# A graph network's fused build-and-update stage: the known half of the update is copied into the PSUM bank ahead of the products that add to it, and the relu reads the bank

## What is computed

```
h = relu(layernorm(x))
# block 0, message passing
m   = relu([h[src], h[dst], edge_attr] @ mW1 + mb1) @ mW2 + mb2
agg = segment_sum(m, src)
u   = relu([h, agg] @ uW1 + ub1)              # the stage of this change
x   = x + h + (u @ uW2 + ub2)
# block 1, three graph convolutions with the same edges and self loops
h = relu(layernorm(x))
x = x + gcn(gelu(gcn(gelu(gcn(h, W1, b1)), W2, b2)), W3, b3)
```

## Time and profile before

| | us |
|---|---|
| median of 3 runs | 2052.21 |
| lowest and highest run | 2049.65, 2060.61 |
| profiled execution | 2049.62 |
| its span, first to last instruction | 2047.8 |
| `build_and_update` in it | about 1218 to 1529 |
| `graph_layers` in it | about 1529 to the end |

### The profile page before, as it was taken

One profiled execution on the slowest core, in us unless ns is written; L12 is line 12 of the kernel. 1 busy time (PEld: TensorE's weight loads), 2 busy tenths in 40 slices (PEclk: granted clock), 3 DMA queues, 4 the chain that ended last, 5 costly groups with the idle time before them and its releaser, 6 DMA issues. The chain is left out here.

```text
span 2047.8 us, 34486 instructions
## 1 busy us (share of the span) xinstructions
PE 1817.7 (89%) x8786; PEld 1237.3 (60%) x8786; DVE 1542.7 (75%) x4650; ACT 797.9 (39%) x1975; POOL 1262.3 (62%) x1463
## 2 busy tenths in 40 slices
PE   4577887777399999999999998989979999999999
PEld 2344544444255555555555556666657888788887
DVE  7887787777489999999999988988988345445333
ACT  0122222222155665665665656656664112113000
POOL 2777777777788888888888859999979000000000
PEclk7677777888699999999999999999999999999999
DMA  5111111111276766666766785222236344343333
GB/s 163 39 58 51 52 58 58 58 58 56 69 197 195 198 195 195 198 195 195 196 196 194 194 173 163 69 66 68 72 92 185 93 124 124 93 126 121 109 108 110
DMA packets 181705, 254.12 MB, mean 124 GB/s; under 512 B 29244, under 2 KB 144761, under 8 KB 181514
## 3 DMA queue, kind: packets, MB, share of 16 engines
q0 software_dynamic: 47888, 126.25, 22.6%
q1 hardware_dynamic: 104696, 102.31, 16.4%
q10 hardware_dynamic: 28930, 23.35, 3.5%
HBM read 202.35 MB, written 49.37 MB: 123 GB/s over the span
## 5 line engine op out<-in xcount | busy, mean ns | idle before, releaser
L1009 POOL DMA_INDIRECT brow<-B_rows,rows x440 | 467.8, 1063 | 114.9 <-issue 58.4
L380 POOL DMA_INDIRECT src_list<-ring,ring_row x392 | 385.8, 984 | 156.7 <-issue 117.6
L1959 PE MATMUL pO<-F,y 128*128 128x512 f32 x1728 | 431.5, 404 | 4.7 <-DVE y L1770 3.2
L1959 PEld LDWEIGHTS pO<-F,y 128*128 128x128 f32 x1728 | 326.7, 190 | 79.8 <-DVE y L1770 4.0
L1332 POOL TENSOR_SCALAR src_oh<-iota,src_s 128x128 bf16<-128x128 bf16 x426 | 285.1, 685 | 39.9 <-PE pC L1475 21.8
L1059 PE MATMUL pNode<-hid_whole,oh 128*128 128x512 f32 x440 | 228.7, 601 | 4.9 <-DVE sums L1195 4.5
L1125 ACT ACTIVATE turned<-pC 128x256 fp32r<-128x256 bf16 x220 | 84.7, 385 | 279.9 <-PE pC L1038 279.9
L1348 DVE TENSOR_SCALAR dst_oh<-iota_cw,dst_s 128x458 bf16<-128x458 f16 x568 | 181.7, 366 | 0.0
L1061 PE MATMUL pNode<-hid_upper,oh 128*128 128x512 f32 x220 | 175.3, 797 | 0.0
L1475 PE MATMUL pC<-dst_oh,src_oh 128*128 128x458 bf16 x568 | 157.4, 361 | 16.6 <-SPq L1430 8.3
L824 PE MATMUL pP<-U,upto 128*128 128x182 bf16 x385 | 49.6, 280 | 136.4 <-DVE posf L587 136.4
(11 more groups left out here) (306 smaller groups left out, 3413.1 us busy)
## 6 DMA issues: line engine op xcount, KB each, us to landing
raw<-C_rows SPq DMA_DIRECT2D x54, 768.0 KB, 4.4
C_rows<-c_rows ACTq DMA_DIRECT2D x175, 114.5 KB, 1.7
raw_first<-C_rows SPq DMA_DIRECT2D x18, 768.0 KB, 4.4
rows<-src_list SPq DMA_DIRECT2D x110, 100.0 KB, 2.8
brow<-B_rows,rows POOLq DMA_INDIRECT x440, 3.8
U_parts<-part_u SPq DMA_DIRECT2D x25, 256.0 KB, 2.0
B_rows<-bst SPq DMA_DIRECT2D x25, 256.0 KB, 2.1
src_list<-ring,ring_row POOLq DMA_INDIRECT x392, 2.2
```

The costliest lines, as they stand in the source:

```text
L380: nc.gpsimd.indirect_dma_start(dr.src_list[:, :, :].rearrange("p t w -> (p t) w"), bass.IndirectOffsetOnAxis(ap=ring_row[:, k % RING, t:t ...
L1009: nc.gpsimd.indirect_dma_start(brow[:, t % BR, :], None, dr.B, bass.IndirectOffsetOnAxis(ap=rows_i[:, m % LCS, j, 1:2], axis=0)).then_inc( ...
L1959: last = mm(pO[m % 2][half][:, :], y[:, win, part, half * P:(half + 1) * P], F[:, n % FS, :], start=(win == 0 and part == 0), stop=False)
```

## The change

Before the 25 tiles begin, PE opens the bank `pU` with one product of 128x512 (in turn 1 at u = 1), which writes every column of it. Then, for each tile, DVE copies the known half from SBUF into `pU` at u == 3, after the relu of the tile before has read the bank; the products of `hidden` add to what stands in the bank (start=False) and no longer overwrite it; and the relu reads the bank directly. PE's first product of `hidden` waits for the copy (`known_ready`) in place of the relu (`u_ready`). The add at u == 8 is gone.

```diff
+        u_opened = g.sem("u_opened")
+        known_ready = g.sem("known_ready")
@@ vector engine
+                    if u == 3 and 0 <= i - 1 < NW:
+                        w = i - 1
+                        if w == 0:
+                            dve.wait_ge(u_opened, 1)
+                        else:
+                            dve.wait_ge(u_ready, w)
+                        dve.wait_ge(h_in[0 if w < HG else 1], 16 * (HG if w < HG else NW - HG))
+                        v.tensor_copy(pU[:, :].rearrange("p (b n) -> p b n", b=2), known_u(w)).then_inc(known_ready, 1)
@@ vector engine, u == 8
                         dve.wait_ge(u_done, w + 1)
                         if w >= 1:
                             dve.wait_ge(x_done, w)
-                        dve.wait_ge(h_in[0 if w < HG else 1], 16 * (HG if w < HG else NW - HG))
-                        link(v.tensor_tensor(uT.rearrange("p (b n) -> p b n", b=2),
-                                             pU[:, :].rearrange("p (b n) -> p b n", b=2), known_u(w), ALU.add))
-                        v.tensor_scalar(uT, uT, 0.0, None, ALU.max).then_inc(u_ready, 1)
+                        v.tensor_scalar(uT, pU[:, :], 0.0, None, ALU.max).then_inc(u_ready, 1)
@@ tensor engine, hidden
                     pe.wait_ge(at_ready, w + 1)
-                    if w >= 1:
-                        pe.wait_ge(u_ready, w)
-                    else:
-                        pe.wait_ge(steps_ready, 4)
+                    pe.wait_ge(known_ready, w + 1)
                 for k in range(2):
                     last = mm(pU[:, m * P:(m + 1) * P], uw1[:, 2 * (m // 2) + k, (m % 2) * P:(m % 2 + 1) * P],
-                              aggT[:, k * P:(k + 1) * P], start=(k == 0), stop=(k == 1))
+                              aggT[:, k * P:(k + 1) * P], start=False, stop=False, skip_group_check=True)
@@ tensor engine, the turns
+                    if i == 1 and u == 1:
+                        pe.wait_ge(steps_ready, 4)
+                        mm(pU[:, :], fresh[:, 0:P], fresh[:, 0:HID], start=True, stop=True).then_inc(u_opened, 1)
```

## The result

| | before | changed |
|---|---|---|
| median of 19 runs, us | 2053.81 | 2047.67 |
| lowest and highest run | 2048.87, 2060.61 | 2043.72, 2056.90 |
| profiled execution | 2049.62 | 2054.11 |
| first to last step of the stage | 308.6 | 304.5 |

The ratio is 0.997, its 95% interval 0.9957 to 0.9983: 6 us less, 3.5 to 9. That is inside what was forecast, in sign and in size, and less than 0.5%.

The account below looks back on a forecast made before the run. PE, DVE and POOL each near 90% busy, none alone the bound; PE and DVE tied in a loop. Terms -8.9 + 3.8 = -5.1 us gave 2044.5 to 2047.1, forecast 2046 us, range 2038 to 2054.

Parts of the forecast that it names:

- The loop: PE and DVE, one-hots to `update`: path 0.74 us instead of 1.22, capped by PE's idle time, 8.9 us less.
- The copy's price: DVE's 128x512 f32 copy from SBUF into PSUM: 650 ns taken, 450 to 680 kept as bounds.
- The copy's place: Copy at u == 3 delays the one-hots of u = 5 to 7 and `hidden`: 3.8 us given back.
- ACT's floor: ACT's bucket reads, 1.63 us each: a faster PE gains nothing in the tail, only in the 21 updates before.
- The sum: Whole kernel: -8.9 + 3.8 = -5.1 us, forecast 2046 us.
- (A): Rival: DVE's idle time hides the copy wholly and the tail gains too, 2037 to 2042 us; chance 0.22.
- (B): Rival: late one-hots after the copy cost PE about 10 us, the gain is gone, 2050 to 2053; chance 0.16.
- (C): Rival: DVE becomes the bound, all 24 turns pay 0.65 us, slower at 2057 to 2062; chance 0.07.
- (D): Rival: the seed in the bank is overwritten, time equals the forecast's; chance inside the forecast's 0.55.

Follow-up runs that it names:

- the relu alone: Changed kernel without the copy into the bank and the product that opens it, known half left out of the result: stage 301.1 us, ratio 0.9972.
- the copy alone: Kernel before, add kept, plus a DVE copy into the bank at u == 3 that the products overwrite: stage 314.4 us, ratio 1.0029.
- seven steps of lead: DVE's one-hots 7 steps ahead of PE in place of 5: stage 302.3 us in the changed kernel, 308.3 in the one before.
- half the copy: Kernel before, add kept, plus a copy at u == 3 of the first 256 columns only, overwritten by the products: stage 311.2 us.
- the copy at u == 1: Changed kernel with copy at u == 1, relu ahead of the one-hots of u == 8, one-hots 7 steps ahead: stage 295.6 us, ratio 0.9936.

## Why the prediction was right, and where it was not

- *The loop.* 0.48 us a turn was worked out, from 1.22 to 0.74; the turn shown has 0.72, and unit 0 is shorter by 0.46. The relu at 675 ns was read from the copy of the same size and is 675. Capped turn by turn by PE's idle time it was to give 8.9 us over 21 updates, which are those of turns 2 to 22; in these turns the relu alone gives 8.5 (239.8 to 231.3). The cap was the right tool, and 0.4 us too generous. (A 22nd, that of turn 23 at 1484.6 us, also lies before the 1485 us that the prediction names; with it its rule gives 9.4.)
- *The copy's price.* 650 ns taken, 681 measured, just over the row of 674 that was the upper bound.
- *The copy's place.* That it is paid in units 4 to 7, and not out of DVE's 28 us of idle time, is shown by the copy alone. Both ways that the prediction named are there: the lead of the one-hots, by unit 6, which seven steps bring back; and `hidden`'s wait for the copy, in turns 4 to 9 and 25. How they share the 3 us is not separated, and seven steps of lead do not win them back. The term itself was 3.8 us: in the changed kernel it measures 3.0 in turns 2 to 21 (220.6 to 223.6), against the old loop 5.3. It was near by luck as much as by method, since the same reading missed the copy alone and half the copy by 2 and 1 us, too low both times.
- *ACT's floor.* Shown: the gain ends with turn 22, as read (-5.4 us in turns 2 to 22, +0.1 in the next three), and the tail moves when ACT's work does. That POOL is not the bound shows in the copy at u == 1: the same POOL work fits into 295.6 us. But its wait for PE did not fall by 5 us, it is 22.4.
- *The sum.* -5.1 us; measured -4.1 in the first profile, -5.3 in turns 2 to 25, -6 in the medians (3.5 to 9). The forecast of 2046 stands 1.7 us under the median of 2047.67. A part of that is luck: it lies 6.2 us under the three runs' median of 2052.21, more than the sum, and the 19 runs' median is 2053.81.
- *Wrong in detail.* DVE's wait before L1404 was to fall to 8 to 12 us and is 20.7. Two additions failed. The 0.48 us a turn was taken from it as if the turn became shorter by the whole 0.48, when it became shorter by 0.22 (5.3 us in 24 turns). And the 0.2 us of more work, 5 us in all, hardly shows: DVE's busy time grows by 0.7 us. A copy of 0.68 us adds 0.52 to it in the copy alone (246.3 to 258.7 for 24), since its row overlaps those of its neighbours, and the one-hots became some ns shorter. Of the 5.9 us of idle time that DVE loses in turns 2 to 25, 3.9 go at L1404 (22.6 to 18.7) and 1.4 ahead of the aggregate. The waits for dst_oh were to grow by 2 to 5 us and fell from 6.5 to 5.1, while the lateness that they were to show is there in the starts. The busy time of PE took it in. Turns 2 to 25 of before and changed (length, busy us of PE, PEld, DVE, ACT, POOL, granted clock, DMA):

```profile
1243.07:1515.25 272.18, 251.43 (x1401) 182.40 (x1398) 246.25 (x821) 169.20 (x313) 253.05 (x377) 1.00 0.25 80
```

```profile
1252.99:1519.89 266.90, 254.38 (x1400) 180.35 (x1398) 246.91 (x821) 169.39 (x313) 249.18 (x378) 1.00 0.26 82
```

  PE idles for 20.8 us in the one and 12.5 in the other, 8.2 less, but its busy time grows by 3.0 for the same products: rows that overlapped lie further apart.
- *The rivals.* (A) fell by the tail and by the copy's cost. (B) and (C) had the mechanism of the copy alone, where it costs more than half of what the loop gives; in the changed kernel it does not reach that, and `hidden` starts on the copy's end in 7 turns of 24, not in most. (D) would not show in the time, and no row here can tell it.

## What to carry to other kernels

Where two engines follow a hand-written order, an operation's cost is not its length against the idle time of its engine, but its length against the lead of what is queued behind it, and against the moment at which the other engine needs its result: 28 us of idle time did not hide 25 copies of 0.68 us. More lead for the one-hots is no cure by itself, as it puts the copy later. Taking work out of the loop pays at once what the other engine idles there; where it is put next decides how much of that is kept, and here two units earlier, with the relu ahead of the one-hots and seven steps of lead, it was 13 us in place of 4 to 5. Read a gain of 0.3% from the starts within the stage, not from the whole span or from the waits, and stretch by stretch: a turn 0 that was long under a lower granted clock made two steps of lead look worth 2 us.

## What the runs showed of the hardware

- VectorE writes 128x512 f32 from SBUF into PSUM in 681 ns and 128x256 in 414: about the price of reading the same size out of PSUM (674 and 425).
- The same stage repeats to 0.4 us, while the whole kernel before differs by 12 us within its 19 runs, by 18 within 34 of the 35 beside the first experiments, and by some 165 us between two sittings on different chips, nearly all of it in the first stage (547 to 556 us against 677 to 681) and the second (668 to 677 against 704 to 714).
- TensorE's granted clock over the first turn, after idle time, differs between kernels whose PE instructions there are the same. It is 0.70 to 0.72 over 11.5 to 12 us in four profiles, whose turn 0 is the long one (13.0 to 13.5 us), and 0.83 or more over 9.8 to 10.8 us in ten (12.1 to 12.3 us). The three kernels that were profiled twice repeat it: 0.84 and 0.84, 0.72 and 0.72, 0.84 and 0.83.
